# Feature rows of a recommendation tower: scaled and summed before the embedding, variance by a Gram matrix, buffers for all gathers

## What is computed

```python
x = layer_norm(dense_t @ Wd.T, gd, bd)                        # 512 x 128
y = layer_norm(einsum('bnd,ed->bne', e, Ws), gs, bs)          # 26 rows of 128 a sample
y = layer_norm(einsum('bne,pn->bep', y, Wsi), gsi, bsi)       # over p = 32
T = concatenate([x[:, None], swapaxes(y, 1, 2)], axis=1)      # 33 x 128 a sample
Z = einsum('bnd,bmd->bnm', T, T)
out = layer_norm(Z[:, TRIL_I, TRIL_J] @ Wl.T, gl, bl)         # 512, the first 384 are used
h = relu(concatenate([out[:, :384], dense_t]) @ W1 + b1); h = relu(h @ W2 + b2); y = h @ W3
```

## Time and profile before

| | us |
|---|---|
| median of 3 runs | 218.5 |
| lowest, highest | 217.47, 221.31 |
| profiled execution, span from first to last instruction | 265.1 |
| TensorE busy in it | 184.7 (70%) |
| ScalarE busy | 145.7 (55%) |
| VectorE busy | 128.7 (49%) |
| GpSimd busy (104 gathers) | 101.8 (38%) |

### The profile page before, as it was taken

The page is one execution under the profiler, slowest core; times in us unless marked ns, Lnnn a source line. Parts: engine busy times, 40 slices in busy tenths (PEclk is TensorE's granted clock), DMA queues, the critical chain, the costliest instruction groups (busy, mean ns, idle before and its releaser), DMA issues.

```text
span 265.1 us, 5053 instructions
## 1 busy us (share of the span) xinstructions
PE 184.7 (70%) x1804; PEld 134.3 (51%) x1804; DVE 128.7 (49%) x388; ACT 145.7 (55%) x585; POOL 101.8 (38%) x108
## 2 busy tenths in 40 slices
PE   0468302027977496787798698889899799886865
PEld 0346301013246275574556597555698466762363
DVE  5804000013279735969543467954367964683000
ACT  0255001028357856676768657886988797740132
POOL 4877777716172724745474455640000000000000
PEclk9999955556997957759999899999999999997999
DMA  6465112104310100111110001110000000000000
GB/s 163 122 157 171 41 25 64 29 11 113 119 20 10 27 10 17 26 18 22 22 22 16 19 20 23 24 20 0 0 0 2 3 2 1 4 5 3 0 2 0
DMA packets 7765, 8.97 MB, mean 34 GB/s; under 512 B 3617, under 2 KB 4769, under 8 KB 7746
## 3 DMA queue, kind: packets, MB, share of 16 engines
q0 software_dynamic: 3328, 3.41, 6.9%
q1 hardware_dynamic: 4418, 5.31, 6.8%
HBM read 8.59 MB, written 0.00 MB: 32 GB/s over the span
## 4 chain that ended last, share of the span: by engine, by line
PE 46%; issue 20%; ACT 15%; DVE 10%; another core or an unknown queue 8%; ACTq 0%; DVEq 0%
PE pU L324 11%; PE pT L369 10%; DVE zr L568 6%; PE pY L300 5%; PE pZ L315 5%; PE pU L343 3%; ACT yn L440 3%; PE pU L408 3%; ACT junk L456 2%; PE pV L343 2%; PE pU L350 2%; ACT znT L495 1%; PE pU L328 1%; DVE t L579 1%
## 5 line engine op out<-in xcount | busy, mean ns | idle before, releaser
L279 POOL DMA_INDIRECT rows<-in_tables,idx x104 | 101.6, 977 | 74.4 <-PE pY L304 35.6
L369 PE MATMUL pT<-wexp,yn 128*128 128x192 f32 (+4 forms) x256 | 53.7, 347 | 9.1 <-issue 8.0
L369 PEld LDWEIGHTS pT<-wexp,yn 128*128 128x128 f32 x256 | 44.2, 224 | 15.9 <-issue 11.2
L300 PE MATMUL pY<-wsc,rowsT 128*128 128x256 f32 x96 | 37.6, 480 | 17.9 <-issue 15.9
L579 DVE SCALAR_TENSOR_TENSOR t<-pT,cols,bias 128x512 f32<-128x512 f32 x32 | 23.7, 740 | 29.3 <-remote 25.8
L440 ACT ACTIVATE yn<-pY,yrs 128x128 f32<-128x128 f32 x96 | 29.9, 366 | 11.6 <-DVE yrs L555 8.4
L324 PE MATMUL pU<-wg,zr 128*128 128x512 f32 x64 | 32.2, 628 | 3.7 <-DVE zr L568 3.3
L464 ACT COPY rowsT<-pY 128x128 f32<-128x128 f32 x48 | 12.0, 251 | 39.5 <-remote 21.9
L300 PEld LDWEIGHTS pY<-wsc,rowsT 128*128 128x128 f32 x96 | 19.4, 235 | 26.2 <-issue 25.8
L315 PE MATMUL pZ<-T 128*32 128x34 f32 x1024 | 18.8, 204 | 19.8 <-issue 19.7
L568 DVE COPY zr<-zs 32x128 f32<-32x128 f32 x128 | 29.5, 231 | 1.7
(11 more groups left out here) (98 smaller groups left out, 203.2 us busy)
## 6 DMA issues: line engine op xcount, KB each, us to landing
wl_sb<-in_wl SPq DMA_DIRECT2D x4, 512.0 KB
rows<-in_tables,idx POOLq DMA_INDIRECT x104
w_sb<-in_w SPq DMA_DIRECT2D x5, 256.0 KB
dense_sb<-in_dense_t SPq DMA_DIRECT2D x1, 512.0 KB
w_sb<-in_w SPq DMA_DIRECT2D x1, 512.0 KB
z<-zs SPq DMA_DIRECT2D x32, 4.0 KB
wsi_sb<-in_wsi_rows SPq DMA_DIRECT2D x1, 208.0 KB
wd_sb<-in_wd_t SPq DMA_DIRECT2D x1, 128.0 KB
```

The lines of the kernel that those rows point to most:

```text
L279: pool.indirect_dma_start(out=rows[:, c // 2, (c % 2) * D:(c % 2 + 1) * D], out_offset=None, in_=tables, in_offset=bass.IndirectOffsetOnAx ...
L300: mm(embedded(j), rowsT[:, j, :], wsc[:], start=True, stop=True).then_inc(y_done, 1)
L369: got = mm(pT[m % 2][:, PJ * (a - SBANK * m):PJ * (z + 1 - SBANK * m)], yn[:, j, c % 2, :], wexp[:, c % TW, a - lo:z + 1 - lo, :], start=f ...
```

## The change

A block is now cut into four units (`UNITS`) of 16 samples in each of its two halves of 64; a unit has 4, 3, 3 or 3 pairs of chunks, one chunk of each half. All loops are unrolled: every engine goes through 16 units (`NU`) in an order of its own.

- `rows` holds the rows of all four blocks; no gather waits for anything but the index. There are still 104.
- The row variance no longer comes from the embedded row: the transposed rows are multiplied with the block-diagonal Gram matrix of centred `Ws` (`gbd`, 128 columns a pair), VectorE multiplies the result with the rows, sums over 64 and clamps at zero; root and reciprocal follow, and VectorE scales the 64-wide rows.
- The sum over features is done on these (`mix`: two products with 64 weight columns, one per half, where one had 128). ScalarE copies the bank, and `embed` applies `Ws` with `gs` folded in: two products a unit, contraction 64, 512 wide.
- Bias, squares, variances and normalising follow for two halves of a unit; `interact` makes the same 32 small products a unit.
- `zs` is laid out so that it goes to DRAM and comes back as `zr` and `z9` by SyncE's DMAs; only the last unit is copied by VectorE and ScalarE (`relaid`: 12 + 8 and 4 copies). The upper products read `zr` with a stride of eight elements.
- `gl` and `bl` are folded into `W1` and `b1` ahead; transposes, layers and answer all use `pU`. The dense part is done before the first unit. Weights are loaded earlier.

The core of the diff (in `block_at(n, lag)` the block k is the one whose first unit was `lag` steps ago; `U0, U1, MLP, TOP` = 6, 7, 8, 9; `LAST` = 3):

```diff
+def last_pair(m):
+    return (US * NF * (m + 1) - 1) // P
+def unit_pairs(m):
+    return range(last_pair(m - 1) + 1 if m else 0, last_pair(m) + 1)
...
-        rows = sb("rows", [P, NPAIR, 2 * D])
+        rows = sb("rows", [P, NBLK * NPAIR, 2 * D])
+        zscr = nc.dram_tensor("zscr", (2, UNITS, P, ZF), F32, kind="Internal").ap()
...
+            for n in range(NU - 1):
+                k, m = divmod(n, UNITS)
+                if m == 0 and k >= 2:
+                    sp.wait_ge(zr_sb, 16 * 6 * (k - 1))
+                sp.wait_ge(zs_sb, n + 1)
+                sp.dma_start(zscr[k % 2, m], zs[:, n % 2]).then_inc(zw[n % 2], 16)
+                if m == UNITS - 1 or n == NU - 2:
...
+                    src = zscr[k % 2].rearrange("m (s p) f -> p (m s) f", p=PJ)[:, 0:4 * units]
+                    for r in range(4):
+                        sp.dma_start(zr[PJ * r:PJ * (r + 1), 0:4 * units],
+                                     src[:, :, QG * G8 * r:QG * G8 * (r + 1)]).then_inc(zr_sb, 16)
                     for r in range(2):
+                        sp.dma_start(z9[PJ * r:PJ * (r + 1), 0:4 * units],
+                                     src[:, :, G8 * (PJ + r):G8 * (PJ + r + 1)]).then_inc(zr_sb, 16)
...
+            for n in range(NU):
...
+                        pool.indirect_dma_start(
+                            out=rows[:, j, h * D:(h + 1) * D], out_offset=None, in_=tables,
+                            in_offset=bass.IndirectOffsetOnAxis(ap=idx[:, 2 * j + h:2 * j + h + 1], axis=0),
+                        ).then_inc(gathered[n], 16)
...
+            def transposes(n):
+                first, count = unit_rows(n)
+                if n >= 2:
+                    pe.wait_ge(e_mul, n - 1)
+                pe.wait_ge(gathered[n], 32 * count)
+                for j in range(count):
+                    got = nc.tensor.transpose(pA[n % 2][:, P * j:P * (j + 1)], rows[:, first + j, :], ident)
+                got.then_inc(r_done, 1)
+            def gram(n):
+                _, count = unit_rows(n)
+                pe.wait_ge(r_sb, n + 1)
+                for j in range(count):
+                    got = mm(pA[n % 2][:, P * j:P * (j + 1)], rowsT[:, n % 2, j, :], gbd[:], start=True, stop=True)
+                got.then_inc(g_done, 1)
+            def mix(n):
+                m = n % UNITS
+                pairs = unit_pairs(m)
+                pe.wait_ge(s_sb, n + 1)
+                if n:
+                    pe.wait_ge(v_sb, n)
+                for i, j in enumerate(pairs):
...
+                        for h in range(2):
+                            got = mm(pV[(n - m + u) % 2][D * h:D * (h + 1), PJ * (a - US * u):PJ * (z + 1 - US * u)],
+                                     srow[:, n % 2, i, D * h:D * (h + 1)], wexp[:, j, a - lo:z + 1 - lo, :],
+                                     start=first, stop=j == last_pair(u), skip_group_check=True)
+                got.then_inc(v_done, 1)
+            def embed(n):
+                pe.wait_ge(v_sb, n + 1)
+                for h in range(2):
+                    if n:
+                        pe.wait_ge(t1_sb, 2 * (n - 1) + h + 1)
+                    mm(pT[h][:], wscg[D * h:D * (h + 1), :], vsb[D * h:D * (h + 1), n % 2, :],
+                       start=True, stop=True).then_inc(y_done, 1)
+            def interact(n):
+                k = n // UNITS
+                t = tile_T(n)
+                pe.wait_ge(t_sb, 2 * (n + 1))
+                pe.wait_ge(xcol_sb, k + 1)
+                if n:
+                    pe.wait_ge(zs_sb, n)
...
+                got.then_inc(z_done, 1)
...
+            for n in range(NU):
+                transposes(n)
+                if (k := block_at(n, MLP)) is not None:
+                    turn(k)
+                if (k := block_at(n, TOP)) is not None:
+                    hidden2(k)
+                gram(n)
...
+                if (k := block_at(n, U0)) is not None:
+                    upper(k, range(0, 4))
+                if (k := block_at(n, U1)) is not None:
+                    upper(k, range(4, QG + 1))
+                if (k := block_at(n, MLP)) is not None:
+                    hidden1(k)
+                if (k := block_at(n, TOP)) is not None:
+                    answer(k)
+                mix(n)
+                embed(n)
+                if n:
+                    interact(n - 1)
+            turn(LAST - 1)
+            hidden1(LAST - 1)
+            interact(NU - 1)
+            hidden2(LAST - 1)
+            answer(LAST - 1)
+            upper(LAST, range(0, QG + 1))
+            turn(LAST)
+            hidden1(LAST)
+            hidden2(LAST)
+            answer(LAST)
...
+            def turned_rows(n):
+                _, count = unit_rows(n)
+                if n >= 2:
+                    act.wait_ge(g_done, n - 1)
+                act.wait_ge(r_done, n + 1)
+                a.copy(rowsT[:, n % 2, 0:count, :],
+                       pA[n % 2][:, 0:P * count].rearrange("p (j r) -> p j r", r=P)).then_inc(r_sb, 1)
+            def row_deviation(n):
+                _, count = unit_rows(n)
+                act.wait_ge(e_var, n + 1)
+                a.activation(esd[:, 0:2 * count], evar[:, 1, 0:2 * count], ACT.Sqrt, bias=eps[:], scale=1.0).then_inc(e_std, 1)
+            def mixed(n):
+                if n >= 2:
+                    act.wait_ge(y_done, 2 * (n - 1))
+                act.wait_ge(v_done, n + 1)
+                a.copy(vsb[:, n % 2, :], pV[n % 2][:]).then_inc(v_sb, 1)
+            def squares(n):
+                for h in range(2):
+                    act.wait_ge(t1_sb, 2 * n + h + 1)
+                    a.activation(t2[:, h], t1[:, n % 2, h], ACT.Square).then_inc(t_sq, 1)
...
+            def interactions(n):
+                act.wait_ge(z_done, n + 1)
+                if n >= 2:
+                    act.wait_ge(zw[n % 2], 16 * (n // 2))
...
+                a.copy(zs[:, n % 2, PJ * G8:].rearrange("p (q g) -> p g q", g=G8), got[:, :, PJ:]).then_inc(zs_sb, 1)
...
+            for n in range(NU):
+                turned_rows(n)
+                if n % UNITS == 1:
+                    x_columns(n // UNITS)
+                if (k := block_at(n, U0)) is not None:
+                    x_row(k)
+                if (k := block_at(n, MLP)) is not None:
+                    upper_turned(k)
+                if (k := block_at(n, TOP)) is not None:
+                    relu2(k)
+                row_deviation(n)
+                if n:
+                    deviations(n - 1)
+                mixed(n)
+                if (k := block_at(n, MLP)) is not None:
+                    relu1(k)
+                if (k := block_at(n, TOP)) is not None:
+                    answered(k)
+                if (k := block_at(n, U1)) is not None:
+                    upper_norm(k)
+                squares(n)
+                if n:
+                    interactions(n - 1)
+                if (k := block_at(n, U1)) is not None:
+                    upper_scaled(k)
+                if 1 <= n <= 4:
+                    wl_sums(range(2 * n - 2, 2 * n))
+            upper_turned(LAST - 1)
+            deviations(NU - 1)
+            relu1(LAST - 1)
+            x_row(LAST)
+            interactions(NU - 1)
+            act.wait_ge(zs_sb, NU)
+            relaid(NU - 1, 3)
+            relu2(LAST - 1)
+            answered(LAST - 1)
+            upper_norm(LAST)
+            upper_scaled(LAST)
+            upper_turned(LAST)
+            relu1(LAST)
+            relu2(LAST)
+            answered(LAST)
...
+            def row_variance(n):
+                first, count = unit_rows(n)
+                dve.wait_ge(g_done, n + 1)
+                v.tensor_tensor(prod[:, 0:count, :], pA[n % 2][:, 0:P * count].rearrange("p (j r) -> p j r", r=P),
+                                rows[:, first:first + count, :], ALU.mult).then_inc(e_mul, 1)
+                dve.wait_ge(e_mul, n + 1)
+                v.tensor_reduce(out=evar[:, 0, 0:2 * count], in_=prod[:, 0:count, :].rearrange("p j (h d) -> p (j h) d", d=D),
+                                op=ALU.add, axis=AX.X).then_inc(e_sum, 1)
+                dve.wait_ge(e_sum, n + 1)
+                v.tensor_scalar(evar[:, 1, 0:2 * count], evar[:, 0, 0:2 * count], 0.0, None, ALU.max).then_inc(e_var, 1)
+            def scaled_rows(n):
+                first, count = unit_rows(n)
+                dve.wait_ge(e_std, n + 1)
+                v.reciprocal(ers[:, 0:2 * count], esd[:, 0:2 * count]).then_inc(e_rs, 1)
+                dve.wait_ge(e_rs, n + 1)
+                if n >= 2:
+                    dve.wait_ge(v_done, n - 1)
+                v.tensor_tensor(srow[:, n % 2, 0:count, :].rearrange("p j (h d) -> p (j h) d", d=D),
+                                rows[:, first:first + count, :].rearrange("p j (h d) -> p (j h) d", d=D),
+                                ers[:, 0:2 * count].unsqueeze(2).to_broadcast([P, 2 * count, D]), ALU.mult).then_inc(s_sb, 1)
+            def biased(n):
+                if n >= 2:
```

(73 more changed lines are left out.)

714 lines of the change are left out of this document (314 added, 400 removed).

## The result

The changed kernel takes 255.81 us (median of 4 runs: 254.66, 254.89, 256.74, 261.27) beside 218.25 for the kernel before on the same chip: ratio 1.167, 95% interval 1.156 to 1.178, 17% slower. The forecast was 256. Some executions of every kernel here come out longer than its others by 1.5% or more (261.27 is one); ratios leave them out, and where they move a median the counted runs are named. The profiled execution took 254.89 us with a span of 253.1, so 1.8 us lie outside the span.

The account below looks back on a forecast made before the run. The prediction took one unit's serial latency through all engines as the bound: start 21, chain 172.8, weight preparation 10.7, other work 5.2 and end 37.5 make 247.2 us; with 8 to 9 for the clock, 256, range 222 to 280.

Parts of the forecast that it names:

- The idle holes of the profile: Three early holes and the 34-column products' waits, taken as the profiled execution's own; span 265.1 us against a median of 218.5.
- The rival that stretched everything evenly: The profile lengthens all durations alike, so the new chain shrinks by 0.82 to 211 us; chance 0.08.
- One step is one unit's latency: Each engine's loop order makes a step one unit's whole chain: 11.55 us for four pairs, 10.55 for three; 172.8 in all.
- What lies beside the chain: Work outlasting VectorE's part: five upper products 0.4, first dense layer 1.1, scaled copy 0.58; 5 us. Weight preparation: 10.7 us.
- Clock: Idle gaps of 4 us on TensorE in steps 0, 5, 9 and 13 lower its clock, costing 8 to 9 us.
- Mix: The two 64-column halves run beside each other: 1.2 us a unit; in sequence 2.2, 16 us more in all.
- strided weights: Upper products' weight loads reading every eighth element stay hidden under a 0.43 us pass; cost taken as 0.
- DRAM relayout: A unit's write and six reads through DRAM have two steps, 21 us, before the upper part; cost 0.
- the rival of the gathers as limit: Unit latency falls below 8.1 us, so steps follow the gathers: 184 us; chance 0.07.
- Start and end: Before the first unit's chain, dense part and first transposes: 21 us; after step 15, relayout copies and last upper part: 37.5.
- all three stay below 40 us a block: TensorE, ScalarE and VectorE each have under 40 us of work a block, so throughput alone suggests a gain.
- What would show it: Signs of being right: transposes near 21 us, steps of 10 to 12, TensorE's share below 60%, gathers over by 140 us.

Follow-up runs that it names:

- e6: The kernel before with row buffers and semaphores for all 104 gathers and its loop over blocks unrolled; 218.94 us, ratio 1.000 to the kernel before.
- its twin: The kernel before with its loop over blocks unrolled and nothing else changed; 219.49 us, ratio 1.003 to the kernel before.
- e7: The changed kernel's instructions with the row stage one unit ahead of mix and embedding in the engines' loops; 213.97 us, ratio 0.978 to the kernel before.
- e1: The changed kernel with one more unused 512-wide VectorE sum per unit, between the previous unit's variances and the reciprocal; 265.57 us.
- e3: The changed kernel with the previous unit's variances moved behind the scaled rows on VectorE; 262.34 us, ratio 1.194 to the kernel before.
- e8: The changed kernel with three useless 512-wide products ahead of the mix in steps 0, 3, 5, 9 and 13; 250.95 us, ratio 1.148 to the kernel before.
- e4: The changed kernel with the mix's products issued one column half after the other instead of alternating; 271.27 us, ratio 1.237 to the kernel before.
- e5: The changed kernel with row buffers for one block again, later gathers waiting until their slot is read; 258.71 us, ratio 1.169 to the kernel before.

## Why the prediction held, step by step

*The idle holes of the profile are of that execution.* Right: the later profiles of the old order (e6, its twin) don't have them. That the holes summed almost exactly to the difference was partly chance, for 13.7 us of it was longer work on TensorE and not idle time. The rival that stretched everything evenly fell with it: durations of single instructions after are those of before (VectorE's 512-wide ones 695 and 678 ns against the earlier trace rows, ScalarE's square 630 against the earlier trace rows).

*One step is one unit's latency.* Right, and e7 shows it: with the same instructions and the row stage one unit ahead the steps are shorter. Which work makes up this latency was only half right. VectorE's part ends last in the five steps without long fill, as the mix's wait for the scaled rows shows, and in the other eleven the fill does. The forecast's own list had that for two of these kinds of step (0.4 and 1.1 us "out"); my expectations for e1 (0.6 in every unit) and e3 (a gain in every unit) forgot it. e1 met its number because the clock fell as well. The terms of the step shown above: row variance part 1.35 to the clamp (1.30 forecast), variances 1.27 (1.34), mix 1.20. The first embedding half gives its result 1.23 us after the group starts, not 1.0; the two bias steps take 1.29, not 1.48; the interaction copies take 0.31 to the next copy, not 0.75, as the second starts before the first has ended. The difference to 10.55 is 0.2.

*What lies beside the chain.* Too simple. It holds for the upper part: four products nearly hidden, and with the other five a step of 11.59 us where 10.55 + 0.4 + 0.58 was forecast. The step with the first dense layer took 11.83, and 11.55 + 1.1 was forecast. But I named for the weight preparation only its sums on ScalarE and VectorE and left out its products:

```profile
38.42 5.89 PE L363 MATMUL pU<-wl_sb,beye 128*32 128x512 f32 x8
```

```profile
78.41 5.12 PE L379 MATMUL pU<-cols,w_sb 128*128 128x1 f32 x24
```

Both are partly at half clock, stand ahead of the mix and outlast the 3.95 us of VectorE's part. The second group is 24 passes one column wide in a step of 16.3 us, the longest of all. Steps 1 to 4 take 56.2 us, where 3 x 10.55 + 11.55 + 10.7 = 53.9 were forecast.

*Clock.* 8 to 9 us forecast, 2 in each of steps 0, 5, 9 and 13; e8 gives back 4 to 5. The loss is only partly where I put it. Step 5 fits (12.06 us at 0.58, where e8's step 13 takes 10.14 at full clock); steps 9 and 13 are only 0.6 to 0.7 above that; and steps 0 to 4 run at 0.50, 0.77, 1.00, 0.62 and 0.58, the other eleven at 0.93 together.

*Mix, strided weights, DRAM relayout, gathers.* Mix right (e4). The strided load is longer, 316 ns where the old one takes 199, and nearly hidden:

```profile
L319 PEld LDWEIGHTS pU<-wg,zr 128*128 128x128 f32 x64 | 19.5, 316 | 7.5 <-issue 1.7
```

At full clock sixteen passes take 7.23 us, the last one 0.59 of it, so they start 0.44 apart against 0.43; 0.2 us a block. No wait of weight in the steps names a DMA. The last gather starts at 135.2 us, as forecast, and e5 and e6 show that neither kernel needs the buffers; the rival of the gathers as limit is out.

*Start and end.* 23.2 us to the first copy instead of 21: first transposes at 22.04 against "near 21", plus their 1.1 us at half clock, which had no term. End 38.1 against 37.5; in it the relayout copies:

```profile
225.13 2.37 DVE L670 COPY zr<-zs 32x64 f32<-32x64 f32 x12 [6.25 <-ACT zs L486]
...
227.52 1.38 DVE L674 COPY z<-zs 32x8 f32<-32x8 f32 x8
229.16 7.23 PE L319 MATMUL pU<-wg,zr 128*128 128x512 f32 x16 [1.45 <-DVE z L674]
```

3.75 us on VectorE, 4 forecast.

*Sum.* 23.2 + 191.8 + 38.1 = 253.1 us of span. The forecast had 21 + 197.7 (with 9 for the clock) + 37.5 = 256, and none of it for the 1.8 us outside the span. The eleven later steps came out some 7 us shorter than their terms, the start and steps 0 to 4 each some 2 longer, so that the total met within 1 us is partly luck. Two sums were wrong on the way. The lower end of the forecast's own range, 238, doesn't follow from its terms: 247.2 with a start of 17 instead of 21 is 243. And "all three stay below 40 us a block" isn't so for TensorE by the terms given, up to 36.3 - 2 + 7 = 41.3. Measured are 92.6 us in eleven steps, 33.7 in four, for the mix takes 24.5 us in all where the old sums over the features took 53.7 (49.1 in the twin). Wrong in "What would show it": TensorE's share is 71%, not below 60%; between 92.50 and 215.00, at a clock of 0.93, it is 76%. That line contradicted my own sum of its work, which would also have shown that TensorE's other work can set the mix.

## What to carry to other kernels

Work out how long one item takes through all engines in the order that each engine's loop is written in; if the next item starts only after the last step of this one, that latency is the time of a step, and work removed beside it changes nothing. Putting the first stage one item ahead was worth 42 us here; with 62 us less work on ScalarE but without that order the kernel was 37 us slower. Before a wait is shortened, look in each kind of step for a second one that ends at nearly the same time (other work queued ahead on the engine that receives), and for what the granted clock does in the steps around it. And compare step by step where the clock is alike: e1's total agreed with its forecast, its steps didn't.

## What was not expected

A kernel with 30 more passes on TensorE is 4.9 us faster (e8), and one whose dependence is relaxed is 6.5 us slower (e3); the granted clock of the profiled runs is 0.905 and 0.797 against 0.852. Why it falls at e3's small shift isn't settled. The same fall stands in executions whose steps are in the changed kernel's order: step 10 takes 12.34 us at 0.80 in e5, and step 14 takes 11.88 at 0.86 in e8, where both take 10.32 at full clock. The column halves of the mix overlap only when they are issued alternately: 1.48 us against 2.45 for the same 20 passes. And one profiled execution held some 47 us of idle time that no other execution of that kernel shows; the timed runs beside its span were what gave it away.
